# A residual term moved from VectorE into a TensorE accumulation, in the node units of a four-layer graph network

## The reference

```python
h = maximum(layernorm(x), 0); x = x + L0(h, edge_attr, src, dst)   # attention over edges
h = maximum(layernorm(x), 0); x = x + L1(h, src, dst)              # sum over edges, / sqrt(degree); + h
h = maximum(layernorm(x), 0); x = x + L2(h, edge_index, ...)       # two convolutions with self loops; + h
h = maximum(layernorm(x), 0); x = x + L3(h, edge_index, ...)       # two convolutions with self loops; relu(. + h)
```

## Time and profile before

| what | value |
|---|---|
| median of 3 runs | 2498.05 us (2489.75, 2498.05, 2498.25) |
| the profiled execution | 2492.77 us; its span, first to last instruction, 2491.0 us |
| busy in the span | VectorE 1880.8 us (76%), TensorE 1800.8 (72%), GpSimd 1773.3 (71%), ScalarE 1299.9 (52%) |
| main phase, first scan of each stage (us) | A 579.5, B 843.9, C 1127.4, D 1420.4, E 1696.7, F 1987.3 |
| from scan to scan in a group with one tick (us) | A 9.85, B 12.04, C 11.31, D 11.35, E 11.31, F 11.51 |
| first DMA of the final scatter | 2227.3 us |

### The profile page before, as it was taken

The page is one execution under the profiler, slowest core; times in us unless marked ns, Lnnn a source line. Parts: engine busy times, 40 slices in busy tenths (PEclk is TensorE's granted clock), DMA queues, the critical chain, the costliest instruction groups (busy, mean ns, idle before and its releaser), DMA issues.

```text
span 2491.0 us, 25939 instructions
## 1 busy us (share of the span) xinstructions
PE 1800.8 (72%) x6414; PEld 870.1 (35%) x6414; DVE 1880.8 (76%) x3066; ACT 1299.9 (52%) x2694; POOL 1773.3 (71%) x1776
## 2 busy tenths in 40 slices
PE   3888888855995788878888878868888888860000
PEld 1433344322543344434444334333444344430000
DVE  6999998647888578987999789887999799960000
ACT  2767676524885455545666456546666566630000
POOL 6777777767777777727776377747777377777776
PEclk9999999877998899979999899879999899985555
DMA  3344433234775454434444356654444354440000
GB/s 70 97 127 128 127 115 89 71 93 146 239 242 185 128 165 124 127 112 104 120 120 118 96 165 188 183 172 107 124 116 123 104 136 134 132 140 22 23 22 20
DMA packets 223225, 302.21 MB, mean 121 GB/s; under 512 B 78896, under 2 KB 85165, under 8 KB 222952
## 3 DMA queue, kind: packets, MB, share of 16 engines
q1 hardware_dynamic: 166632, 249.64, 30.8%
q0 software_dynamic: 56448, 50.92, 11.1%
HBM read 156.13 MB, written 144.91 MB: 121 GB/s over the span
## 4 chain that ended last, share of the span: by engine, by line
DVE 21%; PE 18%; POOL 18%; issue 13%; ACT 6%; DMA 1%; DVEq 0%; POOLq 0%; SPq 0%; ACTq 0%
POOL mn_ring L527 10%; POOL out_dram L1883 8%; PE bank L1195 5%; DVE mn_total L1573 5%; DVE node_h L1401 4%; PE bank L1199 3%; PE bank L1204 3%; PE bank L1927 3%; PE bank L1189 2%; DVE node_h L1446 2%; PE bank L1209 2%; DVE mn_scaled L1589 1%; ACT node_square L1322 1%; ACT node_std L1306 1%; DVE node_x L1425 1%
## 5 line engine op out<-in xcount | busy, mean ns | idle before, releaser
L527 POOL DMA_INDIRECT mn_ring<-slot_rows,addr_i x980 | 969.6, 989 | 445.8 <-issue 293.9
L1195 PE MATMUL bank<-node_x,center 128*128 128x512 f32 x492 | 251.8, 626 | 75.9 <-DVE node_h L1401 71.7
L1204 PE MATMUL bank<-node_h,wconv 128*128 128x512 f32 x492 | 268.3, 628 | 0.3 <-DVE mn_sums L1713 0.3
L1199 PE MATMUL bank<-node_square,mean 128*128 128x512 f32 x492 | 265.3, 622 | 3.7 <-ACT node_std L1301 3.0
L527 POOL DMA_INDIRECT found<-node_table,look_i x196 | 209.4, 1068 | 74.9 <-issue 62.8
L1322 ACT ACTIVATE node_square<-bank 128x512 f32<-128x512 f32 x246 | 145.9, 593 | 210.7 <-PE bank L1195 210.6
L1316 ACT ACTIVATE node_act<-bank,bias 128x512 f32<-128x512 f32 x246 | 168.4, 685 | 148.7 <-PE bank L1204 148.5
L527 POOL DMA_INDIRECT xin<-in_x_dram,src_i x192 | 194.6, 1013 | 64.3 <-issue 57.6
L1883 POOL DMA_INDIRECT out_dram<-keep,scat_i x196 | 193.5, 987 | 62.6 <-issue 62.6
L527 POOL DMA_INDIRECT xin<-in_x_dram,dst_i x192 | 196.0, 1021 | 58.5 <-issue 58.5
L1209 PE MATMUL bank<-node_act,wconv 128*128 128x512 f32 x442 | 229.5, 602 | 2.5 <-ACT node_act L1316 2.5
(11 more groups left out here) (337 smaller groups left out, 3820.8 us busy)
## 6 DMA issues: line engine op xcount, KB each, us to landing
out_dram<-node_rows SPq DMA_DIRECT2D x98, 256.0 KB
mn_rin<-res SPq DMA_DIRECT2D x96, 256.0 KB, 3.8
slot_rows<-node_rows SPq DMA_DIRECT2D x96, 256.0 KB
slot_rows<-keep SPq DMA_DIRECT2D x96, 256.0 KB, 2.0
mn_fcol<-f_rows SPq DMA_DIRECT2D x192, 128.0 KB, 4.0
res<-mn_x SPq DMA_DIRECT2D x72, 256.0 KB, 3.0
node_x_in<-in_x_dram SPq DMA_DIRECT2D x64, 256.0 KB, 3.0
mn_ring<-slot_rows,addr_i POOLq DMA_INDIRECT x980
```

The source lines that it names most:

```text
L527: return eng.indirect_dma_start(out=dest, out_offset=None, in_=table, in_offset=bass.IndirectOffsetOnAxis(ap=index, axis=0))
L1195: pe.matmul(bank[i][:, :], C["center"][:, :], src, start=True, stop=True).then_inc(s["centered"][i], 1)
L1199: pe.matmul(bank[4][:, :], C["mean"][:, :], nd.square[:, i - 1, :], start=True, stop=True) \
L1204: pe.matmul(bank[5 if i == 2 else 1][:, :], C["wconv"][:, 2 * i - 4, :], nd.h[i][:, u % 2, :], start=True, stop=True) \
```

## The change

TensorE adds `h2` to bank 5 by a second product, of `h2` with the identity matrix, that accumulates onto `conv2(2)`. VectorE's operation `res = x2 + h2` is dropped with its buffer and its semaphore, and the operation that makes `x3` takes `x2` where it took `res`. Since `x2` is now read one tick later, it has three buffers in place of two, and ScalarE's copy into it waits for `x3` of the unit three before in place of `res`. `h2` is now also read by the new product, so the wait before it is overwritten is on `conv2(2)` and no longer on `conv1(2)`.

```diff
     def conv2(i, u):
         pe.wait_ge(s["act"][i], u + 1)
-        pe.matmul(bank[5 if i == 2 else 1][:, :], C["wconv"][:, 2 * i - 3, :], nd.act[i][:, 0, :], start=True, stop=True) \
-            .then_inc(s["conv2"][i], 1)
+        if i == 2:
+            pe.matmul(bank[5][:, :], C["wconv"][:, 1, :], nd.act[2][:, 0, :], start=True, stop=False)
+            pe.matmul(bank[5][:, :], C["ident"][:, :], nd.h[2][:, u % 2, :], start=False, stop=True) \
+                .then_inc(s["conv2"][2], 1)
+            return
+        pe.matmul(bank[1][:, :], C["wconv"][:, 3, :], nd.act[3][:, 0, :], start=True, stop=True) \
+            .then_inc(s["conv2"][3], 1)
...
-            need(act, s["res"], u - 1)
-            act.activation(nd.x2[:, u % 2, :], bank[0][:, :], ACT.Copy).then_inc(s["x2"], 1)
+            need(act, s["x3"], u - 2)
+            act.activation(nd.x2[:, u % 3, :], bank[0][:, :], ACT.Copy).then_inc(s["x2"], 1)
...
-        need(v, s["conv1"][i], u - 1)
+        need(v, s["conv2" if i == 2 else "conv1"][i], u - 1)
...
         if 0 <= t - 2 < n:
-            u = t - 2
-            h = normalise(2, u)
-            v.wait_ge(s["h"][2], u + 1)
-            v.wait_ge(s["x2"], u + 1)
-            v.tensor_tensor(nd.res[:, u % 2, :], nd.x2[:, u % 2, :], h, ALU.add).then_inc(s["res"], 1)
+            normalise(2, t - 2)
         if 0 <= t - 3 < n:
             u = t - 3
             v.wait_ge(s["conv2"][2], u + 1)
-            v.wait_ge(s["res"], u + 1)
+            v.wait_ge(s["x2"], u + 1)
             need(v, s["centered"][3], u - 2)
-            v.scalar_tensor_tensor(nd.x3[:, u % 3, :], bank[5][:, :], C["bias"][:, 1:2], nd.res[:, u % 2, :],
+            v.scalar_tensor_tensor(nd.x3[:, u % 3, :], bank[5][:, :], C["bias"][:, 1:2], nd.x2[:, u % 3, :],
                                    ALU.add, ALU.add).then_inc(s["x3"], 1)
```

More of the change, by code:

```diff
@@ L1113, in sb @@
             return ctx.enter_context(K["nc"].sbuf_tensor(f"node_{name}", [P, r, shape], F32))
-        self.x_in, self.x2, self.res, self.x3 = sb("x_in", 3), sb("x2", 2), sb("res", 2), sb("x3", 3)
+        self.x_in, self.x2, self.x3 = sb("x_in", 3), sb("x2", 3), sb("x3", 3)
         self.h1, self.cent = sb("h1", 1), sb("cent", 1)
@@ L1121, in __init__ @@
         self.mean, self.var, self.lnv, self.rstd = (sb(a, 1, 8) for a in ("mean", "var", "lnv", "rstd"))
-        self.s = sems(K["nc"], ctx, "node", "loaded:3 turned x2 res x3 y x4 outT out_rows stored:4 centered:n "
+        self.s = sems(K["nc"], ctx, "node", "loaded:3 turned x2 x3 y x4 outT out_rows stored:4 centered:n "
                       "squared:n var:n std:n rstd:n h:n conv1:n act:n conv2:n local_t:4 local_rows:4 mean1 cent1 x2_rows")
@@ L1280, in third @@
         if 0 <= t - 1 < n:
-            center(2, nd.x2[:, (t - 1) % 2, :], s["x2"], t - 1)
+            center(2, nd.x2[:, (t - 1) % 3, :], s["x2"], t - 1)
         if local(t - 5):
```

## The result

The change makes the kernel slower: 2530.27 us median (2529.19 to 2532.41, 4 runs) against 2498.15 us (2489.75 to 2499.78, 4 runs), ratio 1.0136, 95% interval [1.0113, 1.016]. That holds for the chip on which the kernel before was profiled; on others the totals differ (see the experiments). The profiled execution took 2531.13 us, its span 2529.3: 38.3 more than the span before, where the sum had forecast 44.3.

What follows compares the result with a forecast made beforehand. Bound by a chain across engines in which x3 waits for TensorE's conv2(2) in C and E. Terms 35.0 + 7.5 - 7.1 - 0.6 + 9.5 = +44.3 on 2492.8 give 2537.1, plus 4: 2541 us, range 2522 to 2562.

Steps and rivals of the forecast that it cites:

- The chain and the price: In C conv2(2) on TensorE releases x3; the new product costs 0.86 us, so x3 starts 1.92 us behind conv2(2).
- Rival 1: VectorE's queue sets the tick: 0.61 us gained per tick in C, E, B and F, -43.9 us, 2452; chance 0.07.
- C and E, 17.5 each: Stages C and E: tick 11.31 to 12.17 us, 21 ticks 18.1, less 0.61 at the start; group 24 hidden.
- A, +7.5: Stage A: 19 ticks +0.66 us, mostly hidden by look-ups, leaving 5.8; last two ticks add 1.7.
- B, -7.1: Stage B: x3 waited behind `res`, so it starts 0.47 us earlier in each of 15 ticks.
- D, -0.6: Stage D: ticks shorten, but GpSimd is the limit; only the one tick behind its last gathers counts.
- F, +9.5: Stage F: 14 ticks +0.60 us (8.4), two further ticks +1.7, first tick -0.6; later ticks hidden behind GpSimd.
- Rival 4: GpSimd hides more: A's 5.8 us vanishes behind look-ups, B gives 0.61 a tick; -7.9, 2533; within the forecast's 0.75.

Runs made afterwards that it cites:

- both halves alone: Two edits of the kernel before: `res` dropped without the product, ratio 1.0022, again 0.9881; product added with `res` kept, ratio 0.9852, again 0.9938.
- the form by stage: Kernel before, changed by stage: A VectorE adds h2 and x2; B, D product behind conv2(2); C, E, F product first. 0.9866 third chip, 1.0022 fourth.

## Why the prediction was right, point by point

- **The chain and the price.** Right. x3 is 1.92 behind `conv2(2)` wherever it waits for the product, the product costs 0.86 there, and both halves alone do what the step said. VectorE's idle in front of x3 grew by 1.58 us in C (1.94 - 0.36), forecast 1.47. Rival 1 falls, and for C with it the rule of the Trainium skill (Perfetto Trace Analysis, Identifying the Most-Contended Engine: relieve the engine with the highest occupancy first): VectorE, at 89% the fullest engine, was relieved alone, and C didn't move. It isn't wrong everywhere: in B, where VectorE didn't wait in front of x3, the same relief made the tick 0.77 shorter.
- **C and E, 17.5 each.** 15.2 and 16.7. Three sizes were off. The tick grew by 0.80, not 0.86: it was 11.31 up to group 16 in C (17 in E) only and 11.25 behind it, and the 0.06 are an instruction of VectorE that ran longer before (last section). 21 ticks gave +17.0 in C and +17.1 in E. The first tick gave more than the 0.6: -3.1 in C, -1.9 in E; in C the wait for the gathers fell from 6.17 to 4.89, and the four records of `center` behind it took 2.69 us and not 3.75 (from 1140.28; the window 1140.2 to 1145.0 of the kernel before has a granted clock of 0.50, so TensorE stood at the lower of its two levels there). The last groups with their two ticks cost +1.3 and +1.4, where I had them hidden.
- **A, +7.5.** 4.0. The tick is right (+0.65 for +0.66). The ticks 2 and 3 got 0.73 and 0.74 shorter, where I had put +0.66 for tick 3 and nothing for 2, and tick 4 grew by 0.14 only: VectorE was ready for the look-ups at 813.36, not 815.5. The look-ups hid 10.5 - 3.5 = 7.0 of the delay (812.81 to 816.28 is 3.5), forecast 6.7; ticks 22 and 23 added 1.3, forecast 1.7.
- **B, -7.1.** -7.1, but as -7.7 in the ticks and +0.6 in group 24.
- **D, -0.6.** -2.7. GpSimd was the limit as said, but its own run got shorter, which is 1.6 of the 2.1 missing: from its first gather to its wait at the end of D, 1400.65 to 1659.25 is 258.6 before, 1412.56 to 1669.53 is 257.0 after. The mean gather instruction took 1020 ns before and 1008 after in a window of D.
- **F, +9.5.** +11.4. Groups 1 to 14 gave +9.0 (+9.3 forecast), the first tick +0.5 for -0.6. Ticks 124 and 125 grew by 0.86 each, which I had left out as hidden behind GpSimd; 0.8 of it came back later.
- **The end.** +44.3 against +38.3; 2541 against 2530.27, inside the range. Of the 10.7 us, 6 are the sizes above; the rest is the step from a span to the median, for which I added 4, and the changed kernel's profiled run lies 0.9 above its median.
- **Rival 4** names the sign of the error and hardly its cause: the look-ups hid 0.3 more than forecast, not 5.8, and B's tick of group 20 gave 0.45, not 0.61. The misses of A, C, D and E add up to -8.7 us, and 2.7 came back in F and ahead of A, so that the sum is only 6.0 off is partly luck.

## What to carry to other kernels

The fullest engine isn't the one to relieve if it waits at the place where the work is taken out; look at the idle in front of the next instruction that uses the result. A product that accumulates needn't stand behind the one it adds to: if its operand is early, it can open the bank where TensorE waits anyway, and the same edit can be right in one stage and wrong in the next. Where a chip adds waits of its own, compare ticks, not totals.

## What the runs showed of the hardware that I had not expected

- **Chips differ by a quarter.** The kernel before took 2498.15 us on the first chip and 3118 to 3138 on three others. There ScalarE, which has no wait without a name in the first profile, has 289 of them with 753 us in all (kernel before, fourth chip). Some are ordinary waits whose releaser the profile lost; the 100 of over 2 us make 600 us. The Trainium skill (Runtime: NRT & Kernel Launch, Instruction fetch mechanics) says that each engine streams its instructions in blocks of 256 over a DMA queue of its own while it executes, and calls the cost mostly hidden. Late blocks would fit waits of all engines for no semaphore, but the traces speak against them. The DMA queues for instructions (packets, MB, share) in the profile of that run:

```profile
q8 instruction: 56, 0.92, 0.1%
q14 instruction: 89, 0.73, 0.1%
```

The first chip's profile counts the same 56 and 89 packets. Of ScalarE's 100 long waits 22 hold the end of one of them, and with the packets shifted in time at random it is 22 on average as well. Nor is it TensorE's clock: in stage C of the form by stage on the third chip all ticks of 11.9 had a granted clock of 1.00 (long ticks, 17 to 19 us, had 0.73 to 0.91 on the fourth, kernel before). The cause stays open, and so does why one kernel's ticks are hit and another's not.
- **0.06 us from an overlap.** In stage C of the kernel before, h1 (L1446) started 0.01 to 0.04 us ahead of a gather instruction of GpSimd (1211.86 and 1211.88) in 15 ticks in a row and took 0.74 to 0.76 us; when GpSimd was idle (1370.04) it took 0.69. Over the whole trace the 35 of its 64 instructions with such a start took 0.74 to 0.76, the other 29 took 0.69, also where a gather overlapped them otherwise. After the change it is 0.69 in 62 of 64, and the two of 0.72 and 0.73 are the two that a gather met within 0.01 us. No run moved the gathers alone. A view of that line by itself in the window 1195 to 1385, before and after (count, then shortest, median and longest in ns):

```profile
L1446 DVE SCALAR_TENSOR_TENSOR node_h<-node_cent,node_rstd x17: 692/744/758, 1200.6 to 1381.3; 128x512 f32<-128x512 f32 x17
```

```profile
L1447 DVE SCALAR_TENSOR_TENSOR node_h<-node_cent,node_rstd x16: 691/692/693, 1199.1 to 1380.8; 128x512 f32<-128x512 f32 x16
```

The tick of 11.31 us was nine steps of GpSimd's 1.25 to 1.26, so that the two met at the same place each time; 12.11 isn't such a multiple.
